# Local attention on one core: both tiles' inputs transposed together in every second slot

## What is computed

```python
h = shift_token(x)                      # second half of the channels from the token before
q, k, v = jnp.split(h @ wqkv, 3, axis=-1)
q = l2norm(q) * qs;  k = l2norm(k) * ksc          # per head: 8 heads of 64
q, k = rotary_xpos(q, k)
...
bq = q.reshape(b, h, w, WINDOW, d) * QK_SCALE     # windows of 64 tokens
bk, bv = (look_around(bk), look_around(bv))       # own window and the one before
sim = jnp.where(mask, -jnp.finfo(sim.dtype).max, jnp.einsum('bhwid,bhwjd->bhwij', bq, bk))
o = jnp.einsum('bhwij,bhwjd->bhwid', jax.nn.softmax(sim, axis=-1), bv)
x = x + o.transpose(0, 2, 1, 3).reshape(b, n, INNER) @ wo
```

## Time and profile before

| | |
|---|---|
| median of 3 runs | 1808.47 us (1808.35 to 1809.93) |
| the profiled execution | 1807.17 us |
| its span, first to last instruction | 1805.4 us |
| mean granted TensorE clock | 0.979 |
| busy share of the span: PE, DVE, ACT, POOL | 93%, 80%, 72%, 57% |
| local attention of the first layer, about | 397 to 935 us |
| of the second layer, about | 1100 to 1645 us |

### The profile page before, as it was taken

One profiled execution on the slowest core, in us unless ns is written; L12 is line 12 of the kernel. 1 busy time (PEld: TensorE's weight loads), 2 busy tenths in 40 slices (PEclk: granted clock), 3 DMA queues, 4 the chain that ended last, 5 costly groups with the idle time before them and its releaser, 6 DMA issues. The chain is left out here.

```text
span 1805.4 us, 54585 instructions
## 1 busy us (share of the span) xinstructions
PE 1683.2 (93%) x18244; PEld 1157.7 (64%) x18372; DVE 1446.0 (80%) x3283; ACT 1298.3 (72%) x3588; POOL 1036.9 (57%) x1015
## 2 busy tenths in 40 slices
PE   4999999958999999999979997999999999996997
PEld 2666666635777777777755664677777777764654
DVE  1777777768899999999957775899999999984997
ACT  3888888837988989898962223888989898983221
POOL 0333333327777777777743323777777777772564
PEclk9999999979999999999998998999999999998999
DMA  4111111121111111111113321111111111112343
GB/s 109 51 47 46 49 53 47 41 56 31 42 36 41 44 41 35 43 42 43 34 42 87 95 76 36 34 45 41 35 43 42 43 33 44 41 39 65 107 125 86
DMA packets 209335, 94.05 MB, mean 52 GB/s; under 512 B 90818, under 2 KB 200300, under 8 KB 209260
## 3 DMA queue, kind: packets, MB, share of 16 engines
q1 hardware_dynamic: 209260, 93.09, 19.7%
HBM read 51.03 MB, written 25.23 MB: 42 GB/s over the span
## 5 line engine op out<-in xcount | busy, mean ns | idle before, releaser
L821 ACT ACTIVATE pr<-banks,nb,rr 128x128 f32<-128x128 f32 x1024 | 455.8, 465 | 4.8 <-DVE nb L890 4.8
L726 POOL TENSOR_TENSOR rr<-ss,half_neg 128x16 f32<-128x16 f32 x128 | 374.3, 2924 | 19.0 <-POOL ss L723 17.0
L743 POOL TENSOR_TENSOR pr<-pr,rl 128x512 f32<-128x512 f32 x256 | 266.1, 1040 | 101.3 <-DVE rl L852 101.3
L860 DVE TENSOR_REDUCE ss<-sq 128x16 f32<-128x1024 f32 x128 | 156.1, 1220 | 76.6 <-ACT sq L770 63.8
L821 ACT ACTIVATION_READ_ACCUMULATOR pr<-banks,nb,rr 128x1 f32 x1024 | 217.4, 212 | 0.0
L1190 ACT ACTIVATE f_g<-banks,b_s 128x512 f32<-128x512 f32 (+1 forms) x96 | 65.8, 686 | 199.8 <-PE banks L1274 190.6
L868 DVE TENSOR_REDUCE mx<-banks 128x8 f32<-128x1024 f32 x128 | 156.0, 1218 | 8.2 <-PE banks L992 7.4
L370 POOL TENSOR_SCALAR a_ve<-a_mv 128x2 f32<-128x2 f32 x96 | 21.1, 220 | 232.0 <-DVE a_mv L381 228.9
L949 PE MATMUL banks<-ident,pr 128*128 128x128 f32 x1024 | 140.8, 280 | 5.9 <-POOL pr L743 5.9
L734 POOL TENSOR_TENSOR krot<-ka,rr 128x512 f32<-128x512 f32 x128 | 133.4, 1043 | 22.4 <-POOL rr L726 11.7
L812 ACT COPY pT<-banks 128x512 f32<-128x512 f32 x128 | 75.0, 586 | 96.1 <-PE banks L949 96.1
(11 more groups left out here) (124 smaller groups left out, 4250.5 us busy)
## 6 DMA issues: line engine op xcount, KB each, us to landing
ve<-vt SPq DMA_DIRECT2D x128, 128.0 KB, 2.2
hs<-y_d SPq DMA_DIRECT2D x128, 64.0 KB, 1.9
yt<-y_d SPq DMA_DIRECT2D x64, 128.0 KB, 2.1
y_d<-yn SPq DMA_DIRECT2D x64, 128.0 KB, 2.0
f_h<-y_d SPq DMA_DIRECT2D x128, 64.0 KB, 2.0
f_y<-y_d SPq DMA_DIRECT2D x64, 128.0 KB, 2.2
xa<-in_L_attn_x SPq DMA_DIRECT2D x32, 128.0 KB, 2.1
xr<-in_L_attn_x SPq DMA_DIRECT2D x32, 128.0 KB, 2.3
```

The lines of the kernel that those rows point to most:

```text
L726: nc.gpsimd.tensor_tensor(rr[:, r, :], ss[:, r, :], half_neg[:], ALU.pow).then_inc(T["rr"], 1)
L743: nc.gpsimd.tensor_tensor(pr[:, e], pr[:, e], rl[:, e].unsqueeze(2).broadcast_to([P, UH, P]), ALU.mult).then_inc(T[("ne", "no")[e]], 1)
L821: a = nc.scalar.activation(pr[:, e, j, :], bank[e][:, j * P:(j + 1) * P], ACT.Exp, bias=nb[:, X.t, UH * e + j:UH * e + j + 1], scale=rr[:, ...
L860: nc.vector.tensor_reduce(ss[:, 2 * X.p + X.t, :], sq[:].rearrange("p (h d) -> p h d", d=DH), AX.X, ALU.add).then_inc(T["ss"], 1)
```

## The change

`hT` gets a second half, by the parity of the batch. In the first slot of a step `turn_h` transposes both tiles of the batch into two parts of bank 5 and counts once, and ACT copies the 256 columns at once; in the second slot neither is called. The waits follow: the h loads and the projection of q count batches, the projection waits for `hT` only for the first tile, ACT waits for an older projection of v before it writes, and `out_project` waits for the residual of the tile before in the second slots, where no `turn_h` has waited for it.

```diff
--- before.py
+++ after.py
@@ -317,7 +317,7 @@
 
         hs = sb("hs", [P, 2, TPB, D])
         yt = sb("yt", [P, 2, TPB, D])
-        hT = sb("hT", [P, TPB, P])
+        hT = sb("hT", [P, 2, TPB, P])
         sq = sb("sq", [P, 2 * INNER])
         ss = sb("ss", [P, 2 * TPB, 2 * HEADS])
         rr = sb("rr", [P, 2 * TPB, 2 * HEADS])
@@ -675,7 +675,7 @@
 
             def load_h(b, q):
                 n = l * B + b
-                until(sp, T["hT_ps"], 2 * n - 2)
+                until(sp, T["hT_ps"], n - 1)
                 for c, row in ((0, 1), (1, 0)):
                     sp.dma_start(hs[:, q, :, 64 * c:64 * c + 64],
                                  y_d[2 * l][bass.ds(b, 1), row:row + N, 64 * c:64 * c + 64].rearrange(
@@ -772,9 +772,9 @@
             def turned_h(X):
                 if not X.live:
                     return
-                act.wait_ge(T["hT_ps"], X.x + 1)
-                until(act, T["v_ps"], X.x - 1)
-                nc.scalar.copy(hT[:, X.t, :], bank[5][:, 0:P]).then_inc(T["hT"], 1)
+                act.wait_ge(T["hT_ps"], X.n + 1)
+                until(act, T["v_ps"], X.x - 2)
+                nc.scalar.copy(hT[:, X.p].rearrange("p t n -> p (t n)"), bank[5][:, 0:N]).then_inc(T["hT"], 1)
 
             def values(X):
                 if not X.live:
@@ -831,7 +831,8 @@
                 nc.scalar.copy(kT[:, X.p, :, 1 - X.t, :], bank[3][:].rearrange("p (j n) -> p j n", n=P)
                                ).then_inc(T["kT"], 1)
 
-            turned_h(Tile(l, i, p, s, 0))
+            if s == 0:
+                turned_h(Tile(l, i, p, s, 0))
             weighed(Tile(l, i, p, s, 4))
             turned_even(Tile(l, i, p, s, 3))
             turned_odd(Tile(l, i, p, s, 3))
@@ -953,7 +954,7 @@
                 if not X.live:
                     return
                 passed_tile(pe, T["qs"], X, 1)
-                nc.tensor.matmul(v_bank(X)[:], hT[:, X.t, :], wqkv_s[:, l, 2 * INNER:],
+                nc.tensor.matmul(v_bank(X)[:], hT[:, X.p, X.t, :], wqkv_s[:, l, 2 * INNER:],
                                  start=True, stop=True).then_inc(T["v_ps"], 1)
 
             def turn_h(X):
@@ -961,7 +962,9 @@
                     return
                 pe.wait_ge(T[f"h_in{X.p}"], 32 * half_count(X.n))
                 until(pe, T["yn"], X.x - 4)
-                nc.tensor.transpose(bank[5][:, 0:P], hs[:, X.p, X.t, :], ident[:]).then_inc(T["hT_ps"], 1)
+                for t in range(TPB):
+                    m = nc.tensor.transpose(bank[5][:, t * P:(t + 1) * P], hs[:, X.p, t, :], ident[:])
+                m.then_inc(T["hT_ps"], 1)
 
             def turn_odd(X):
                 if not X.live:
@@ -1002,9 +1005,10 @@
             def project_q(X):
                 if not X.live:
                     return
-                pe.wait_ge(T["hT"], X.x + 1)
+                if X.t == 0:
+                    pe.wait_ge(T["hT"], X.n + 1)
                 until(pe, T["ks"], X.x)
-                nc.tensor.matmul(q_bank(X)[:], hT[:, X.t, :], wqkv_s[:, l, 0:INNER],
+                nc.tensor.matmul(q_bank(X)[:], hT[:, X.p, X.t, :], wqkv_s[:, l, 0:INNER],
                                  start=True, stop=True).then_inc(T["q_ps"], 1)
 
             def turn_q(X):
@@ -1027,16 +1031,15 @@
                 if not X.live:
                     return
                 until(pe, T["v"], X.x - 1)
-                nc.tensor.matmul(k_bank(X)[:], hT[:, X.t, :], wqkv_s[:, l, INNER:2 * INNER],
+                nc.tensor.matmul(k_bank(X)[:], hT[:, X.p, X.t, :], wqkv_s[:, l, INNER:2 * INNER],
                                  start=True, stop=True).then_inc(T["k_ps"], 1)
 
             def out_project(X):
                 if not X.live:
                     return
                 pe.wait_ge(T["oT"], X.x + 1)
-                passed_tile(pe, T["hT"], X, 4)
-                if isinstance(X.x, int) and X.x + 4 >= X.end:
-                    pe.wait_ge(T["yn"], X.x)
+                if X.t == 1 or (isinstance(X.x, int) and X.x + 4 >= X.end):
+                    until(pe, T["yn"], X.x)
                 for c in range(4):
                     m = nc.tensor.matmul(bank[5][:, 0:D], oT[:, X.t, c, :], wo_s[:, l, c, :],
                                          start=(c == 0), stop=(c == 3))
@@ -1067,7 +1070,8 @@
                 until(pe, T["pTo"], X.x - 1)
                 turn(krot[:, X.t], bank[3], T["kT_ps"])
 
-            turn_h(Tile(l, i, p, s, 0))
+            if s == 0:
+                turn_h(Tile(l, i, p, s, 0))
             scores(Tile(l, i, p, s, 2))
             turn_even(Tile(l, i, p, s, 3))
             turn_odd(Tile(l, i, p, s, 3))
```

## The result

The changed kernel takes 1812.66 us, the median of 13 runs (1811.92 to 1815.15), against 1809.94 (1806.55 to 1811.49) in 13 runs of the kernel before. The ratio on record is 1.0023, with a 95% interval of 1.0015 to 1.0030; the quotient of the two medians alone is 1.0015. The interval leaves out 1, so the kernel is slower, by little. Forecast were 1812.2 and slower as the likeliest side. The profiled execution took 1813.94 us around a span of 1812.1, at a mean granted clock of 0.978.

The account below looks back on a forecast made before the run. PE's order was taken to bound the attention steps, with second-slot scores waiting for kT. Loops 2.9, unrolled batches 0.3 and stage starts 0.5 us made +3.7, taking the 1808.47 median to 1812.2; range 1806.5 to 1816.0.

Parts of the forecast that it names:

- (a): PE, second slot: the transpose of h goes, with two waits.
- (b): PE, first slot: a second transpose behind the first adds 0.11 us; at most the same comes back in the second.
- (c): Second slot's scores wait for kT, so an odd batch gets back 0.08 us against 0.11 added: +0.03.
- (d): Loop's kT copy can start 0.07 us later, uncovered without turn_h in even batches: +0.08 each; upper end 0.095 a batch.
- (e): ACT's hT copies: 256 columns take 0.40 us, 0.10 more in the first slot, up to 0.30 less in the second; hidden.
- (f): What follows in the first slot comes 0.11 us later without loss; what is late next is kT.
- (g): Waits and queues of out_project, the h loads and the second half of hT: nothing for all three.
- (h): Start of each stage: second transpose and longer copy delay the first project_q by 0.25 us; bounds 0 and 0.3 a layer.
- (A): The forecast: kT's way to the scores limits every second slot; +2.4 to +6 us, chance of more than +3.6: 0.5.
- (B): Same kT limit without the loop's extra 0.07 us: +2.4, 1810.9 us; chance 0.25 with the low part of (A).
- (C): Nothing changes: a transpose costs the same in either slot and kT comes in time; -0.9, 1807.6 us; chance 0.17.
- (D): Faster: the slot pays for going over to turn_h, 62 steps lose it once; -12, 1796 us; chance 0.08.

Follow-up runs that it names:

- two_waits_fewer_late_kt: Changed kernel without ACT's second wait before the kT copy and DVE's before nb, kT waited for between the mask matmuls: 1808.24 us, ratio 0.9993.
- one_wait: Changed kernel without ACT's second wait (for scores of two tiles before) ahead of the kT copy: 1813.62 us, ratio 1.0017.
- two_waits_fewer: Changed kernel without ACT's second wait ahead of the kT copy and without DVE's second wait ahead of nb: 1811.60 us, ratio 1.0013.
- late_kt_after: Changed kernel with the scores' wait for kT moved between the two mask matmuls: 1813.15 us, ratio 1.0017.
- late_kt_before: Kernel before the change with the scores' wait for kT moved between the two mask matmuls: 1806.36 us, ratio 0.9986.
- counted: Changed kernel with an increment on each of the two transposes of h and the waits counting tiles: 1813.47 us, ratio 1.0024.
- idle_turn: Changed kernel with a transpose nobody reads at turn_h's old place in each second slot: 1815.03 us, ratio 1.0031.
- add_alone: Kernel before the change with an unused transpose added ahead of turn_h in the first slot, turn_h kept in both slots: 1815.43 us, ratio 1.0030.
- wait_order: Changed kernel with the two waits ahead of ACT's kT copy swapped: 1813.14 us, ratio 1.0023.
- shifted: Changed kernel with both transposes of h and the wide copy in the second slot, for the next batch: 1814.29 us, ratio 1.0022.

## Why the prediction was right, point by point

The side and the mechanism hold, and the time lies 0.5 us from the median; part of that nearness is luck. The looped steps cost 4.7 us where I had 2.9, and the time was forecast from a median of three runs, 1808.47, that lies 1.5 below the median of thirteen; the difference of the two medians is 2.7 us, not my 3.7.

**(a), (b)** hold: the second transpose costs 0.11 in the first slot, and at two_waits_fewer_late_kt's 16.353 the exchange is even. **(c)** holds: the distance without stall is 0.86 to the first mask matmul, the path over kT needs 0.88, and the written-out batches became 0.02 longer (forecast 0.03). They are three a layer rather than the five of the sum, and the last step of each layer became 0.09 shorter (16.27 to 16.18), so that term is nothing instead of +0.3.

**(d) is the term that was mis-sized.** I had "+0.03" for the odd batch and "+0.08" for the even one. Measured: +0.096 and +0.084. For the even batch the size was right, though the cause was twofold: the wait of two steps on ACT and, at nearly the same time, ACT's own order behind a late `nb`; one_wait took the first away and gained 0.004, two_waits_fewer took both and gained 0.091. For the odd batch I had carried over the 0.31 of its first slot before. In the changed program the copy at the end of that slot has the 0.38, which one_wait shows by removing it: 16.449 to 16.373. The mean over both batches, 0.090, lies near the upper bound of (d), 0.095. I had treated the late start as a property of the batch. It is one of each copy, by what carries its wait, and the trace before showed it elsewhere too: the copy at the end of the second slots starts 0.38 behind the last transpose (its four transposes start at 509.62 and take 0.66, 0.27 of it the last one's own, so that starts at 510.01) in all 52 looped steps, where `turn_h` just covered it:

```profile
510.39 0.59 ACT L831 COPY kT<-banks 128x512 f32<-128x512 f32 x1
```

In the kernel after these copies have the 0.31, and those of all first slots start 0.38 to 0.39 behind. Why the built program puts a register instruction here and not there stays open.

**(e)** holds. The wide copy took 0.41 (estimated 0.40); this is the line of ACT's groups in the steady part of the kernel after (busy us, mean ns, idle before):

```profile
L777 ACT COPY hT<-banks 128x256 f32<-128x256 f32 x25 | 10.3, 410 | 0.0
```

**(f)** holds for the rows that it names. "What is late next is kT" was too short: behind kT comes krot, which holds the steps of late_kt_after at 16.40 instead of 16.35. In the kernel after itself, at 16.45, the wait for kT is the longer one. **(g)** holds, PE has no new wait but that of L985. **(h)**: the chain is as I said and a little longer. From the first transpose of h to the first `project_q` it takes 1.20 and 1.17 us in the two layers, against 0.88 and 0.84 before: 0.32 where I had 0.25, above my bound of 0.3. Whether it reaches the time stays open: the first scores stand at 414.0 us after against 412.8 before, but at 414.4 in late_kt_before, whose start is unchanged.

**The rivals.** (A) it was, at the upper part of its range. (B), odd steps without the 0.07, is what one_wait half gives: 16.373. (C) is excluded by the 0.09 a step; its condition, a kT in time, is met in two_waits_fewer_late_kt, where it comes true. (D) would have needed less than 1.08 from `project_v` to the masks, and 1.18 is what stands there. The runs speak against the rule of the increments too: in `counted` 64 increments more left both steps as they were to the last thousandth. By the Trainium skill, "TensorE: Matmul & The Clock Gate", section "The cost: per-tile semaphore tail", an increment more a step would have made an estimated 0.026 of each; `counted` doesn't show it.

## What to carry to other kernels

Before work is taken off a full engine in one slot and put into another, look at what the work covers where it stands: it is only given back if nothing else arrives at the same time, and here the kT copy arrived with nothing to spare in one step and 0.03 us late in the next. A filler on the full engine (idle_turn) and the addition alone (add_alone) tell in two runs whether a place is limited by the engine or by an arrival. Then shorten the arrival: put a wait on the last instruction that needs it, and drop waits that another one implies.

## What was not expected of the hardware

A second wait that can't be the last still costs time if it pushes the wait that is the last one off the instruction that does the work. ACT starts its kT copy 0.31 us behind PE's last transpose where the copy itself carries the wait, 0.36 where an instruction that only waits stands ahead of it (wait_order, in the loop and in the written-out steps), and 0.38 where a register instruction carries it; DVE starts `nb` 0.04 and 0.12 us behind the maxima. one_wait and two_waits_fewer show the price by leaving one wait out: 16.449 against 16.373 in odd steps, and both together 16.464 against 16.373 in even ones, 4.3 us of the 4.7 that the looped steps had lost. Which instruction of the built program carries a wait changed with edits elsewhere (after and shifted have the late copies in other slots than before), and no run here shows what decides it.
